# A cross-attention and expert kernel: GpSimd's norm written as a product and a sum, rho sums of two tanh blocks issued together, and the hand-placed steps set anew

## The reference

```python
n1 = layernorm(x)                                  # over 256
txt = ctx @ Ws ; feat = n1 @ W                     # ctx: (4, 77, 256)
h   = tanh(txt[:, None, :, :] + feat[:, :, None, :] + b)   # (4, 1024, 77, 256)
rho = h @ w + mask ; att = softmax(rho)            # over the 77
t   = att @ ctx
x   = x + tanh(t @ Wcw + bcw) * n1 + tanh(t @ Wcb + bcb)
n2  = layernorm(x)
probs = softmax(n2 @ gate)                         # 8 experts
each expert takes its 512 best tokens of 4096: gelu(tok @ W1 + b1) @ W2 + b2, times its score
x   = x + sum over experts + gelu(n2 @ Ws1 + bs1) @ Ws2 + bs2
```

## Time and profile before

| | us |
|---|---|
| median of 3 runs (935.6, 943.54, 935.0) | 935.6 |
| the profiled execution's own time | 938.19 |
| its span, first to last instruction | 936.5 |
| busy: PE / PEld / DVE / ACT / POOL | 820.0 / 479.3 / 711.6 / 766.1 / 349.6 |

### The profile page before, as it was taken

How to read it: one execution, slowest core, us unless ns; L and a number is a source line. 1 busy time by engine, 2 the same in 40 slices (tenths; PEclk the granted TensorE clock), 3 DMA queues, 4 the chain that set the end, 5 groups by cost and what they waited for, 6 DMA issues and landing times.

```text
span 936.5 us, 14102 instructions
## 1 busy us (share of the span) xinstructions
PE 820.0 (88%) x5379; PEld 479.3 (51%) x5379; DVE 711.6 (76%) x1406; ACT 766.1 (82%) x596; POOL 349.6 (37%) x533
## 2 busy tenths in 40 slices
PE   6775678667999998889999899997898999999995
PEld 4321122213444443434444455554676888888885
DVE  5689879997979599977979885866785676666540
ACT  4889998999999999999899999893741576676671
POOL 2410650819632018765005910063202155555432
PEclk9899999999999999999999999999899999999998
DMA  8000000000001000200000100003104165544522
GB/s 261 10 1 1 1 1 1 10 14 20 5 1 45 1 1 23 69 1 1 23 1 1 46 24 1 23 1 112 46 1 135 46 181 135 134 108 117 133 23 29
DMA packets 32406, 41.82 MB, mean 45 GB/s; under 512 B 2365, under 2 KB 29011, under 8 KB 32339
## 3 DMA queue, kind: packets, MB, share of 16 engines
q1 hardware_dynamic: 26083, 32.49, 10.3%
q0 software_dynamic: 6144, 8.39, 5.4%
q10 hardware_dynamic: 112, 0.04, 0.0%
HBM read 28.33 MB, written 12.58 MB: 44 GB/s over the span
## 4 chain that ended last, share of the span: by engine, by line
PE 52%; POOL 14%; DVE 14%; ACT 12%; issue 5%; DMA 1%; ACTq 0%; POOLq 0%; DVEq 0%
PE bank L750 12%; PE bank L876 10%; ACT z L957 10%; PE bank L899 9%; DVE z L1310 8%; PE bank L801 8%; POOL xn L1080 5%; PE bank L786 5%; PE bank L726 2%; PE bank L679 2%; POOL scale L1139 2%; PE bank L914 1%; PE bank L774 1%; POOL y_ry L1073 1%; POOL y_ra L1071 1%
## 5 line engine op out<-in xcount | busy, mean ns | idle before, releaser
L957 ACT ACTIVATE z<-z 128x4096 f32<-128x4096 f32 (+5 forms) x157 | 522.1, 3363 | 21.9 <-DVE z L1310 21.7
L1310 DVE TENSOR_SCALAR z<-feat,txt_bias 128x1024 f32<-128x1024 f32 (+1 forms) x716 | 422.6, 660 | 34.5 <-PE bank L750 34.2
L750 PE MATMUL bank<-z,window 128*32 128x512 f32 x2464 | 311.3, 610 | 60.0 <-ACT z L957 59.0
L750 PEld LDWEIGHTS bank<-z,window 128*32 128x32 f32 x2464 | 68.9, 111 | 244.8 <-issue 144.7
L801 PE MATMUL bank<-ws_sb,u 128*128 128x256 f32 x512 | 131.0, 399 | 0.0
L801 PEld LDWEIGHTS bank<-ws_sb,u 128*128 128x128 f32 x512 | 95.1, 195 | 40.5 <-issue 26.8
L786 PE MATMUL bank<-tr,ws_s 128*128 128x512 f32 x384 | 108.3, 419 | 0.1
L876 PE MATMUL bank<-xg_s,w_s 128*128 128x512 f32 x384 | 99.2, 396 | 1.5 <-issue 1.5
L1205 POOL DMA_INDIRECT xg<-xn_dram,idx x32 | 37.9, 1185 | 142.5 <-DVE score L1609 135.2
L899 PE MATMUL bank<-w_s,hid_s 128*128 128x256 f32 x672 | 89.0, 281 | 0.0
L899 PEld LDWEIGHTS bank<-w_s,hid_s 128*128 128x128 f32 x672 | 86.4, 188 | 4.9
(11 more groups left out here) (235 smaller groups left out, 769.3 us busy)
## 6 DMA issues: line engine op xcount, KB each, us to landing
w_raw<-in_L_ffn_W_dram SPq DMA_DIRECT2D x16, 1024.0 KB, 5.8
x_ring<-in_x_dram SPq DMA_DIRECT2D x8, 512.0 KB, 7.9
xn_dram<-xn SPq DMA_DIRECT2D x8, 512.0 KB, 2.9
out_dram<-x_ring SPq DMA_DIRECT2D x8, 512.0 KB, 3.7
u<-in_L_ffn_Ws_dram SPq DMA_DIRECT2D x1, 1024.0 KB, 12.8
ws_sb<-in_L_ffn_Ws_dram SPq DMA_DIRECT2D x1, 1024.0 KB, 15.4
xg<-xn_dram,idx POOLq DMA_INDIRECT x32, 6.1
out_dram<-y,idx POOLq DMA_INDIRECT x32
```

The costliest lines, as they stand in the source:

```text
L750: ins = e.matmul(sums[v][32 * r:32 * r + 32, :], window[:, c, 31 - k:63 - k], z[:, n % ZB, at_piece:at_piece + TOK], start=(v, r) not in b ...
L957: e.activation(part, part, ACT.Tanh).then_inc(signal(*step), 1)
L1310: ins = e.tensor_scalar(z[:, n % ZB, i * width:(i + 1) * width], feat_of(units, c), bias_of(units, t, c), None, ALU.add)
```

## The change

The steps and their arithmetic stay the same but for these:

- `normalise` on GpSimd first forms offset = -(mean * factor) in two instructions of 128x4, and then the four instructions multiply by the factor and add the offset. VectorE's own `normalise` stays.
- `TOGETHER = 2`: rho(n) of an even n is held back and emitted together with rho(n+1), except at the last block of a unit, where what is held is emitted at once. What lies in slot n of an even n now stands ahead of rho(n).
- `B2_ROWS` goes from 64 to 128: the bias matmuls run over 128 rows, the added ones zero.
- `picked` and `fold` become float32r.
- `SPLITS` of the last batch goes from 7 to 5, `DIRECT_EVERY` from 16 to 18, and the tables of places and fills get other numbers.

```diff
--- before.py
+++ after.py
@@ -26,36 +26,37 @@
 BASE, TOP = 16512, 229344
 
 
-SPLITS = ((8, 20), (0, 20), (0, 20), (0, 7))
+SPLITS = ((8, 20), (0, 20), (0, 20), (0, 5))
 FIRST_DIRECT = (4, 3, 3, 3, 2, 2, 2, 2)
-DIRECT_EVERY = (16, 1)
+DIRECT_EVERY = (18, 1)
 AHEAD = 3
+TOGETHER = 2
 BUSY = 18
 ENDS_BEHIND = 3
 FFN_STEPS = ("up", "gelu", "down", "down_end", "store_out", "load_x")
 
-PRE_FIRST = (0, 0, 1, 2, 2, 3, 3, 4, 5, 6, 6)
-PRE_EARLY = (18, 19, 19, 22, 23, 23, 25, 25, 27, 29, 30)
-PRE_LATE = (26, 27, 28, 31, 32, 32, 33, 33, 35, 36, 38)
-TAIL_EARLY = (0, 0, 1, 3, 3, 4, 5, 6, 9, 6, 10, 11, 11, 13)
-TAIL_FIRST = (-1, -1, 0, 3, 3, 4, 5, 6, 9, 6, 10, 11, 13, 14)
-TAIL_LATE = (0, 1, 2, 3, 6, 7, 9, 9, 13, 9, 15, 16, 17, 18)
-TAIL_SINGLE = (-1, 0, 1, 2, 3, 5, 6, 7, 10, 7, 10, 11, 12, 12)
+PRE_FIRST = (0, 0, 3, 3, 4, 4, 3, 4, 4, 7, 8)
+PRE_EARLY = (18, 19, 19, 22, 23, 23, 26, 24, 29, 29, 30)
+PRE_LATE = (26, 28, 28, 31, 33, 33, 33, 34, 36, 34, 38)
+TAIL_EARLY = (0, 0, 1, 4, 5, 6, 6, 6, 8, 6, 10, 12, 12, 13)
+TAIL_FIRST = (-1, -1, 0, 3, 3, 5, 6, 7, 13, 7, 11, 13, 12, 16)
+TAIL_LATE = (0, 1, 2, 4, 7, 10, 12, 10, 16, 11, 17, 18, 19, 22)
+TAIL_SINGLE = (-1, 0, 1, 2, 3, 5, 4, 6, 10, 7, 8, 10, 9, 10)
 
 FFN_PLACES = (-1, 1, 2)
-FFN = ((12, 2.0), (33, 2.3), (14, 2.2), (36, 2.2), (14, 1.5), (26, 1.6))
+FFN = ((9, 2.1), (34, 2.1), (13, 2.2), (36, 2.2), (14, 1.7), (26, 1.6))
 LAG = 2
 BY_VECTOR = ("down_end", "store_out", "load_x")
-B2_ROWS, B2_LOW = 64, 32
+B2_ROWS, B2_LOW = 128, 32
 
 TAIL_FILL = (4, 0)
 KEEP = 8
 READY_FILL = (0, 0)
 TEST_FILL = (2, 4, 3, 2, 1, 2, 1, 3, 2, 0)
-RANK_FILL = (2, 2, 4, 1)
-EXPERT_FILL = (5, 1, 1)
-SECOND_FILL = (5, 6, 1)
-LIST_FILL = (2, 0, 0, 2)
+RANK_FILL = (2, 3, 2, 2)
+EXPERT_FILL = (10, 1, 1)
+SECOND_FILL = (6, 5, 1)
+LIST_FILL = (1, 2, 0, 1)
 PIECES = (4, 2)
 
 SPLIT_TERMS = ((1, 0), (0, 1), (0, 0))
@@ -178,6 +179,7 @@
     def add(n):
         order.append(("add", n))
 
+    summed, unit_ends = [], {*ends_at.values()}
     for n in range(AHEAD - 1):
         add(n)
         if n == 0:
@@ -187,7 +189,11 @@
             add(n + AHEAD - 1)
         if n + 1 < LAST:
             order.append(("tanh", n + 1))
-        order.append(("rho", n))
+
+        summed.append(("rho", n))
+        if n % TOGETHER == TOGETHER - 1 or n in unit_ends:
+            order += summed
+            summed.clear()
         if n < LAST - 1:
             order += slots.pop(n, [])
     last = slots.pop(LAST - 1, [])
@@ -393,7 +399,7 @@
         same_expert = sb("same_expert", [P, P])
         earlier_tile = sb("earlier_tile", [P, P])
         expert_of = sb("expert_of", [P, E])
-        fold = sb("fold", [P, 32])
+        fold = sb("fold", [P, 32], F32R)
         iota_a = sb("iota_a", [P, A])
         tok_part = sb("tok_part", [P, 2])
         tok_tile = sb("tok_tile", [P, NT])
@@ -407,6 +413,7 @@
         x_ve, x_ra = sb("x_ve", [P, J]), sb("x_ra", [P, J])
         x_ry = sb("x_ry", [P, UNITS, J])
         x_sd = sb("x_sd", [P, UNITS, J])
+        offset = sb("offset", [P, J])
         y_ve, y_ra = sb("y_ve", [P, J]), sb("y_ra", [P, J])
         y_ry = sb("y_ry", [P, 2, J])
         scale = sb("scale", [P, 2, J])
@@ -432,7 +439,7 @@
         cnt = sb("cnt", [P, CANDIDATES], BF16)
         same_expert_h = sb("same_expert_h", [P, P], BF16)
         off = sb("off", [P, 4])
-        picked = sb("picked", [P, P])
+        picked = sb("picked", [P, P], F32R)
         V = 5
         pick = sb("pick", [P, NT, 32], BF16)
         vals = sb("vals", [P, NT, E, V], BF16)
@@ -1076,8 +1083,13 @@
                 return ins
 
             def normalise(src, dst, mean, factor):
+
+                link(e.tensor_tensor(offset[:], mean, factor, ALU.mult))
+                e.wait_ge(pool_link, linked)
+                link(e.tensor_scalar(offset[:], offset[:], -1.0, None, ALU.mult))
+                e.wait_ge(pool_link, linked)
                 for j in range(J):
-                    ins = e.tensor_scalar(dst[:, j, :], src[:, j, :], mean[:, j:j + 1], factor[:, j:j + 1], ALU.subtract, ALU.mult)
+                    ins = e.tensor_scalar(dst[:, j, :], src[:, j, :], factor[:, j:j + 1], offset[:, j:j + 1], ALU.mult, ALU.add)
                 return ins
 
             e.memset(ident[:], 0.0).then_inc(consts, 1)
@@ -1620,7 +1632,7 @@
                     e.tensor_tensor(parts[:, 1, :], hid[:, m % HC, :], parts[:, 0, :].bitcast(F32),
                                     ALU.subtract).then_inc(signal(*step), 1)
                 elif kind == "split_b2":
-                    low = slice(B2_LOW, B2_ROWS)
+                    low = slice(B2_LOW, 2 * B2_LOW)
                     e.wait_ge(loaded["b2"], 64)
                     e.tensor_tensor(b2_row[:], ident[0:B2_ROWS, 0:E + 1], ident[0:B2_ROWS, B2_LOW:B2_LOW + E + 1], ALU.add)
                     link(e.tensor_copy(b2_s[:], b2_raw))
```

## The result

Over 13 runs each the changed kernel takes 934.0 us in the median (924.8 to 938.5) and the kernel before 939.9 (935.0 to 943.5). The ratio is 0.994, 95% interval 0.991 to 0.997: a small gain of 0.6%, where 1.9% was forecast. 934 us lies outside the stated range of 907 to 932; the medians differ by 5.9 us where 17.5 were forecast.

A forecast was written before the change was run, and what follows sets the result against it. ACT was taken to bound the kernel up to 636 us, then a chain of small steps to 727, then PE. The terms summed to -17.5 us: 920.7 from the profiled 938.2, 918.1 against the median; likeliest 919, range 907 to 932.

The forecast's parts named there:

- (a): First unit-1 norm: it ends 2.6 us sooner, ACT's first wait goes and the second loses a third; -3.7 us.
- (b): Tanh stage: pairing rho relieves PE by 10 us and shorter norms help, cutting ACT's other 16.4 us of idle time; -6.0 us.
- Rival 1: Pairing delays even blocks' sums and makes ACT wait more, doubling its idle time: +17.6, 953 us; chance 0.11.
- (c): ACT's tanh work: four pair blocks become single ones with a direct piece each, one direct piece less; +0.9 us.
- (d): Unit 6's norm near the last tanh: its transposes come four blocks earlier, so the last rho ends sooner; -1.3 us.
- (e): Unit 7's norm, at 651.59 us, which PE waits for ahead of the first count's total: shorter norm, -1.7 us.
- (f): The two late FFNs: four half bias openings in the chain after 658 us get cheaper, half hidden; -0.8 us.
- (g, h): Experts' 128-row bias openings, 11 x 0.39 us, -4.3; float32r folding matmuls, -0.6; -4.9 us together.
- Fills: PE's filler entries around the first fold: moving them costs and saves an entry's wait; 0 us.
- Rival 3: The exclusive lock at full price: GpSimd's norm gets no faster beside additions; -13.8, 921.8 us; chance 0.07.
- Rival 2: PE's relief and the shorter norms stay hidden, ACT's 24.1 us of idle time remain; -7.8, 927.8 us; chance 0.24.
- two signs of a wrong prediction: The experts' stage no shorter, or the last tanh ending later than some 627 us.

The follow-up runs named there:

- norm_alone: The kernel before with only GpSimd's norm rewritten as a product and a sum; ratio 0.989 to the kernel before.
- norm_bias: The kernel before with the short norm, the 128-row bias and float32r folding, no pairing, old tables; ratio 0.978 to the kernel before, 921.0 us.
- pairs_alone: The kernel before with only the rho sums issued in pairs, old tables, norm and bias; ratio 1.010 to the kernel before.
- after_unpaired: The changed kernel with the pairing taken back (TOGETHER = 1), all else as changed; ratio 0.986 to the kernel before.
- after_turns_behind: The changed kernel, with each even slot that holds transposes of normed rows emitted behind its pair of sums; ratio 0.984 to the kernel before.
- bias_alone: The kernel before with only the bias matmuls over 128 rows and float32r folding; ratio 0.995 to the kernel before.
- norm_bias_pairs: The kernel before with short norm, 128-row bias, float32r folding and rho sums in pairs, old tables; ratio 0.979 to the kernel before.

## Why the prediction was wrong, point by point

**(a) The first norm, -3.7.** Right for the norm: in norm_alone the four first waits are 2.19, 1.02 and 0.83 us, one is gone, 4.0 instead of 7.7. Wrong for the change: the new places of unit 1 turn it back. Its timeline of ACT:

```profile
50.79 2.76 ACT L964 ACTIVATE z<-z 128x3072 f32<-128x3072 f32 x1 [4.77 <-DVE z L1322]
54.34 3.62 ACT L964 ACTIVATE z<-z 128x4096 f32<-128x4096 f32 x1 [0.79 <-DVE z L1322]
```

The first two waits have become one of 4.77 us. With both copies of the features in slot 4, DVE waited 7.0 us for PE at the first, with additions behind it in its queue. They began at 45.3 us, where norm_alone has them at 40.3 and 45.1. Measured -1.0.

**(b) Rho in pairs and the shorter norms, -6.0.** This is the step that failed, and it held two errors of opposite sign.

The first is the norm's price in this stage. It was sought in the relief of PE, with nothing for PE's standing; norm_alone shows -14.5 us up to the last tanh, of which (a) explains 3.7. I had read that DVE waits for PE and had not asked what PE waits for: 24.4 us in ten places for the norm. Not each of these is passed on: after those at 186, 232 and 260 us ACT waits for nothing until 289.8.

The second is the pairing, priced as 10 us less PE work, with nothing for the lateness of its sums. The work got less by 6.0 us up to the last tanh in the changed kernel and by 5.5 on norm_bias, and not at all in pairs_alone, but it was no limit; pairing alone moved the last tanh by +9.7 us (some 7 without its late start) and the changed kernel's by +8.9. Rival 1 named the place (a norm's transposes on top of two slots' work) and gave it 0.11, because it found 7.9 us to spare where 7.0 were needed. That rests on six z buffers; with the four of the kernel it finds 0.6, and the price at nothing has no ground. What the runs put in its place is a mixture: for the larger part, with the long norm or the new tables, the even slot's transposes went ahead of a ready sum and PE stood at them; for the 4 us that pairing costs with the short norm and the old tables, if they are more than spread, the cause stays open.

A smaller misreading: not every idle time of ACT in this stage ends with DVE's addition. Three (0.42, 0.38 and 1.27 us) ended with an `up` matmul, for the `gelu`.

**(c) +0.9.** ACT's busy time up to the last tanh rose by 0.7 us.

**(d) -1.3.** Wrong sign, +1.6. The short norm alone brought -1.6 (3.8 us in norm_alone, from 5.4), with the new tables it was 4.9 us (after_unpaired), and with pairs 7.0. The transposes of unit 6 did come four blocks sooner, but PE stood at them too, and its lag reached the last sums:

```profile
637.86 5.34 PE L757 MATMUL bank<-z,window 128*32 128x512 f32 x36
```

These 36 matmuls, the sums of three blocks in a row, are the order's doing; that they begin 1.6 us behind the last tanh (636.22) is the lag's. In after_turns_behind the same 36 begin 1.4 us ahead of it, and the copy comes 4.0 us behind.

**(e) -1.7.** Measured -0.2. The norm itself is what was forecast, alone 2.16 us for four instead of 4.86, and PE gets it sooner after y_scale; but the second half of the transposes waits for something else (POOL, then PE):

```profile
654.44 2.16 POOL L1092 TENSOR_SCALAR xn<-x_ring,y_ry,offset 128x256 f32<-128x256 f32 x4
...
656.66 0.70 PE L686 MATMUL bank<-ident,xn 128*128 128x128 f32 x4 [0.60 <-POOL xn L1092]
...
659.77 1.08 PE L686 MATMUL bank<-ident,xn 128*128 128x128 f32 x4 [2.41 <-DVE eq L1489]
```

Their bank is the one from which DVE still has to read the low digits (line 1489), a step that lies behind the first count in DVE's queue. Before, it ended at 657.56, while PE was still at the first four transposes for the late norm, so it was not to be seen as a wait. With it moved ahead 17.1 us are left of 17.9, and then ACT's part of the count is the last. So at most 0.8 us were to be had; the prediction had seen ACT's part end 0.9 us before the total and took -1.7 all the same. I had named the step that gets faster and not asked what is late next.

**(f) -0.8.** -1.7 up to expert 0, within what the clock's place does to this stage.

**(g, h) -4.9.** Measured -5.0 in the changed kernel, -4.7 in bias_alone.

**Fills: 0.** No sign of them in the profiles; not tried by themselves.

**Rivals.** Rival 3 (the lock takes the norm's gain) is out: with its two small instructions a norm took 5.0 us beside additions at 30 us and 4.6 at 515 us in the profile after (4.09 and 3.96 for its four large instructions), not 7.1. The page "SBUF — State Buffer" of the Trainium skill, section "SBUF: two separate sides", says that a GpSimd instruction can be blocked for a whole VectorE instruction; the rows agree with waiting (1.0 us beside 0.54 alone) but not with a whole addition of 0.76 for each. Rival 2's figure, 928, is nearest to the time, and its 24 us of idle ACT came out, by a cause that is not its own: norm_alone and pairs_alone show that neither edit is hidden. Two effects that cancel happened to leave the idle time where it was. The two signs of a wrong prediction are split: the experts' stage is shorter, but the last tanh ends at 636.2, not by some 627.

## What to carry to other kernels

When an engine that bounds a stage waits, follow the wait down, engine by engine, to the one that stands for a single late producer, and ask what lies ready behind it in its queue. Here each engine walks through its steps in order, so the producer's latency was paid there, although PE, DVE and GpSimd each had far more idle time in the stage than ACT. Saving that engine some work brought nothing that could be seen; an edit that moves steps ahead of ready work must be priced by what those steps wait for, and by how late the ready work may come. That last number hangs on the count of buffers, which is to be read from the line that sets it and checked against one place of the trace. And a term whose releaser gets faster is worth only the distance to the next releaser of the same instruction.

## What the runs showed of the hardware

- A full array against 64 rows: four matmuls of 256 columns over 64 rows, between others over 128, took 0.65 us, and the twelve behind them 1.62. With half of 128 rows zero it was 0.47 and 1.41, so the 64-row form cost 0.39 us around each opening.
- GpSimd took 2.16 us for four 128x256 product-and-sum instructions and 4.86 for difference-and-product, with both operands per partition and no additions of DVE beside them. Beside additions the first form took 4.0 to 4.1.
- Standing can have a second price: in the place above the granted clock was at its lower level after 3.2 us of waiting, and the next 46 matmul instructions took 9.1 us where they take 6.4 (1.09 and 1.64 in after_turns_behind and 3.64 at 608.54, at the higher level). It is not always so: in norm_bias_pairs PE stood 3.32 us up to 411.2, and the clock was 1.00 from 412.3 to 416 us; in after_turns_behind it stood 3.18 us up to 262.0, the eight transposes took 1.10, and only then did the clock fall, to 0.50 from 263 to 266.
